# Reordering the prologue of a four-layer conditioned sequence kernel: which weights are loaded first, and what waits for them

## The reference

```python
# layer 0
x = x + a_alpha * attention(gamma * rmsnorm(x) + beta)          # 16 heads, softmax
x = x + f_alpha * (silu(h @ gate_w.T) * (h @ hidden_w.T) @ out_w.T + out_b)
# layer 1
u = (x * (scale * rsqrt(ms + EPS))) @ up_w.T; val, gate = split(u)
y = act_quant(val * gelu(gate)) @ weight_quant(down_w).T + x
#   weight_quant(w): s = 1/mean|w|; clip(round(w * s), -1, 1) / s
# layer 2
dWd = ((h_lang @ Wdd.T + bdd) * 0.1).reshape(B, 128, 256)       # per batch
dWu = ((h_lang @ Wdu.T + bdu) * 0.1).reshape(B, 256, 128)
x = x + relu(x @ (Wd + dWd).T + bd) @ (Wu + dWu).T + bu
# layer 3
out = (layernorm(x) * weight + bias + tanh(cond @ lin_w.T + lin_b)) * weight + bias
```

## Time and profile before

| | |
|---|---|
| median of 3 runs | 1004.62 us (1004.0 to 1006.42) |
| profiled execution | 1005.99 us |
| its span, first to last instruction | 1004.2 us |
| PE busy | 954.2 us, 95% of the span |
| VectorE, ScalarE, POOL busy | 745.1, 568.7, 230.8 us |
| mean granted TensorE clock | 0.98 |
| DMA | 89.43 MB, 89 GB/s over the span |

### The profile page before, as it was taken

One profiled execution on the slowest core, in us unless ns is written; L12 is line 12 of the kernel. 1 busy time (PEld: TensorE's weight loads), 2 busy tenths in 40 slices (PEclk: granted clock), 3 DMA queues, 4 the chain that ended last, 5 costly groups with the idle time before them and its releaser, 6 DMA issues.

```text
span 1004.2 us, 20848 instructions
## 1 busy us (share of the span) xinstructions
PE 954.2 (95%) x6574; PEld 782.9 (78%) x6574; DVE 745.1 (74%) x1728; ACT 568.7 (57%) x1167; POOL 230.8 (23%) x303
## 2 busy tenths in 40 slices
PE   6678799999999999999999999999999999998997
PEld 4346569788887979787888979787888979786776
DVE  3844368787878878787878878887878787885756
ACT  2365464756666564756665564746565564745542
POOL 1423502121121312221221312121212213111220
PEclk9789899999999999999999999999999999999999
DMA  8787742130404022130404021130404031120000
GB/s 276 247 284 288 264 166 62 44 106 3 148 1 137 11 85 62 43 105 1 147 1 139 9 95 52 48 100 1 147 1 142 6 104 44 54 84 2 22 16 17
DMA packets 76272, 89.43 MB, mean 89 GB/s; under 512 B 16512, under 2 KB 62864, under 8 KB 73616
## 3 DMA queue, kind: packets, MB, share of 16 engines
q1 hardware_dynamic: 70160, 63.07, 20.7%
q0 software_dynamic: 2304, 16.78, 4.6%
q10 hardware_dynamic: 3776, 9.18, 2.5%
HBM read 63.14 MB, written 25.31 MB: 88 GB/s over the span
## 4 chain that ended last, share of the span: by engine, by line
PE 83%; DVE 6%; DMA 4%; issue 3%; ACT 2%; POOL 0%; SPq 0%; ACTq 0%; DVEq 0%; POOLq 0%
PE bank L709 17%; PE bank L773 14%; PE bank L723 8%; PE bank L668 7%; PE bank L678 6%; PE bank L650 6%; PE bank L623 5%; PE bank L686 3%; PE bank L790 3%; PE bank L632 2%; DMA hyper<-w_hyper 2%; PE bank L602 2%; PE bank L810 1%; PE bank L783 1%; PE bank L695 1%
## 5 line engine op out<-in xcount | busy, mean ns | idle before, releaser
L529 POOL TENSOR_TENSOR act_lo<-act_f,act_hi 128x256 fp32r<-128x256 f32 x120 | 88.3, 736 | 363.6 <-ACT act_hi L1144 363.6
L1412 DVE TENSOR_REDUCE neg_max<-bank 128x2 f32<-128x512 f32 x256 | 162.2, 684 | 0.1
L1101 ACT ACTIVATE probs<-bank 128x512 f32<-128x512 f32 x256 | 134.9, 602 | 26.1 <-PE bank L668 13.6
L1180 ACT ACTIVATE gelu_g<-bank,r 128x256 f32<-128x256 f32 x128 | 60.9, 477 | 94.0 <-PE bank L773 91.4
L709 PE MATMUL bank<-h_hi,gh_hi 128*128 128x256 f32 x512 | 103.4, 283 | 2.8 <-DVE h_lo L1475 2.8
L1138 ACT ACTIVATE silu_g<-bank 128x256 f32<-128x256 f32 x128 | 49.4, 386 | 99.2 <-PE bank L709 98.5
L709 PE MATMUL bank<-h_lo,gh_hi 128*128 128x256 f32 x512 | 103.0, 283 | 0.0
L709 PE MATMUL bank<-h_hi,gh_lo 128*128 128x256 f32 x512 | 102.6, 282 | 0.0
L1481 DVE TENSOR_TENSOR act_f<-bank,silu_g 128x256 f32<-128x256 f32 x128 | 53.8, 421 | 63.8 <-ACT silu_g L1138 63.8
L1144 ACT ACTIVATE act_hi<-act_f 128x256 fp32r<-128x256 f32 x128 | 53.6, 419 | 75.6 <-DVE act_f L1481 73.4
L709 PEld LDWEIGHTS bank<-h_hi,gh_hi 128*128 128x128 f32 x512 | 82.6, 188 | 11.9 <-issue 7.0
(11 more groups left out here) (208 smaller groups left out, 2017.3 us busy)
## 6 DMA issues: line engine op xcount, KB each, us to landing
hyper<-w_hyper POOLq DMA_DIRECT2D x16, 1024.0 KB, 7.1
q_stack<-q_dram SPq DMA_DIRECT2D x96, 128.0 KB
k_stack<-k_dram SPq DMA_DIRECT2D x96, 128.0 KB
q_dram<-probs SPq DMA_DIRECT2D x16, 512.0 KB, 2.8
k_dram<-probs SPq DMA_DIRECT2D x16, 512.0 KB, 2.8
x_res<-xT SPq DMA_DIRECT2D x16, 256.0 KB, 2.8
delta_dram<-hyper_s ACTq DMA_DIRECT2D x15, 256.0 KB, 2.8
out<-xc SPq DMA_DIRECT2D x15, 256.0 KB, 2.5
```

Of the source, the lines that this page charges most:

```text
L529: pool.tensor_tensor(act_lo[:, c % 3, :], act_f[:, c % 2, :], act_hi[:, c % 3, :].bitcast(F32), ALU.subtract).then_inc(g_lo.sem, 1)
L1101: act.activation(probs[:, h % SLOTS], halves(SCORE_BANKS[h]), ACT.Exp, scale=float(H / D) ** 0.5).then_inc(s_exp.sem, 1)
L1180: act.activation(gelu_g[:, n % 2, :], halves(7 - n % 2)[:, 1, :], ACT.Gelu, scale=r3[:, t:t + 1])\
L1412: dve.tensor_reduce(neg_max[:, qt, :, pair:pair + 1].rearrange("p a o -> p (a o)"), halves(n % 3), AX_X, ALU.max, negate=True).then_inc(ma ...
```

## The change

The work itself stays the same. What changes is the order, the queue or the engine:

- **SP's prologue.** The conditioning table is loaded in two pieces, first the 128 KB for the attention's gamma and beta, later the rest. Batch 1's input is loaded into `x1`, which is free at that time, behind the qkv weights. The down weights follow at once. `write_qk` of batch 1 comes ahead of the table's store and no longer waits for it.
- **Key stack of batch 0 on POOL** (`stack_k`, semaphore `first_k_dma`), beside the query stack on SP.
- **Wide weights.** Pieces 0 and 1 are loaded behind both stacks of batch 0; pieces 2 to 5 behind the row of maxima; pieces 8 to 15 by SP instead of POOL, 8 to 11 ahead of the row of maxima of batch 1 and 12 to 15 behind it. Their products stand at other places, and pieces 2, 12 and 13 are evicted by VectorE.
- **Gate weights.** Both are loaded behind the stacks of batch 0 instead of at 10 us. The high part of the first is made in run 0 ahead of the exponentials, the high part of the second by VectorE. The last up weight is loaded in run 1.
- **Row of maxima.** SP issues it in run 0 ahead of the residual input `x_res` and ahead of the wait for the table.
- **Norms.** VectorE normalises batch 0 ahead of the first table steps, and batch 1 ahead of the rest of the table. The sum over the down weights moves ahead of batch 1's norm, its use (mean and reciprocals) behind the 16 maxima of batch 0, and PE's sum over the partitions goes to bank 3.
- **PE.** 6 and 8 products into bank 2 that nobody reads (`keep_busy`) stand ahead of the first norm and behind the first conditioning products. Batch 1's mean stands ahead of the remaining conditioning products.

```diff
@@ -186 @@ landed, by_dve, by_act
-def use(n):
-    return n // 4 if n < 6 else 2 + (n - 6) // 2
+def landed(n):
+    if n >= EARLY + 2:
+        return hyper_late[n % 2].sem, 16 * ((n - EARLY) // 2)
+    return hyper_in[slot(n)].sem, 16 * (n // 4 + 1 if n < EARLY else 3)
+def by_dve(n):
+    return HYPER_DVE.index(n) + 1
+def by_act(n):
+    return len([m for m in range(n + 1) if m not in HYPER_DVE])
@@ -260 @@ semaphores and places
-cond_in, vec_in, small_in, qkv_in, wo_in = sem("cond_in"), sem("vec_in"), sem("small_in"), sem("qkv_in"), sem("wo_in")
+cond_in, cond_late, vec_in, small_in, qkv_in, wo_in = sem("cond_in"), sem("cond_late"), sem("vec_in"), sem("small_in"), sem("qkv_in"), sem("wo_in")
 tanh_act, table, ternary, abs_mm = sem("tanh_act"), sem("table"), sem("ternary"), sem("abs_mm")
-w_hi, w_lo = sem("w_hi"), sem("w_lo")
+w_hi, w_hi_dve, w_lo = sem("w_hi"), sem("w_hi_dve"), sem("w_lo")
 hyper_in = [sem(f"hyper_in{i}") for i in range(4)]
+hyper_late = [sem(f"hyper_late{i}") for i in range(2)]
 EARLY = 6
-BESIDE = (0, 2, 3, 5, 6, 8, 9)
-HYPER_DVE = range(3, 4)
+HYPER_DVE = (2, 12, 13)
+BESIDE = (1, 2, 4, 5, 7, 8)
@@ -288 @@ hyper_load, stack_k
     return cond_dram[:, bass.ds(bat(b), 1), first * DC:(last + 1) * DC].rearrange("p o k -> p (o k)")
+def hyper_load(eng, n):
+    if n >= 4:
+        eng.wait_ge(hyper_mm.sem, n - 3 if n < EARLY else n - 1)
+    eng.dma_start(hyper[slot(n)][:], w_hyper[:, n * HYW:(n + 1) * HYW]).then_inc(landed(n)[0], 16)
         .then_inc(hyper_out[n % 4].sem, 16)
+def stack_k(eng, count):
+    for a in range(2):
+        even = slice(64 * a, 64 * a + 32, 2)
+        odd = slice(64 * a + 1, 64 * a + 32, 2)
+        third = slice(64 * a + 32, 64 * a + 64, 2)
+        for rows_at, part in ((even, 0), (odd, 0), (third, 1)):
+            src = k_dram[:, part].rearrange("(m a r) n -> a r m n", a=2, r=DH)[a]
+            to = k_stack[rows_at].rearrange("r (m a) n -> r a m n", a=2)[:, a]
+            eng.dma_start(to.bitcast(F32), src).then_inc(count.sem, 16)
@@ -374 @@ SP, run
     load_x(nxt)
-if a:
+if a and a.follows():
@@ -400 @@ SP, run, ahead of the row of maxima
         .then_inc(adapt_dma.sem, 16)
+if starts(f):
+    for n in range(8, 12):
+        hyper_load(sp, n)
@@ -408 @@ SP, run, behind the row of maxima
                      max_rows[NPAIR * par:NPAIR * (par + 1), :].bitcast(F32)).then_inc(max_dma.sem, 16)
+if starts(a):
+    sp.wait_ge(cond_out.sem, 16)
+    load_res(a)
+if starts(f):
+    hyper_load(sp, 12)
+    hyper_load(sp, 13)
+    hyper_load(sp, 14)
+    sp.wait_ge(hyper_ev_dve.sem, by_dve(12))
+    hyper_store(sp, 12)
+    hyper_load(sp, 15)
+    sp.wait_ge(hyper_ev_dve.sem, by_dve(13))
+    hyper_store(sp, 13)
 if starts(a):
-    for n in HYPER_DVE:
-        sp.wait_ge(hyper_ev_dve.sem, n - HYPER_DVE[0] + 1)
-        hyper_store(sp, n)
+    sp.wait_ge(hyper_ev_dve.sem, by_dve(2))
+    hyper_store(sp, 2)
@@ -452 @@ SP, prologue
 sp.dma_start(cond_t[C:P, NB:2 * NB], condT).then_inc(cond_in.sem, 16)
-sp.dma_start(cond_w, w_cond).then_inc(cond_in.sem, 16)
+sp.dma_start(cond_w[:, 0:2 * D], w_cond[:, 0:2 * D]).then_inc(cond_in.sem, 16)
 sp.dma_start(w_qkv[:], w_qkvT.rearrange("(c p) n -> p c n", p=P)).then_inc(qkv_in.sem, 16)
+for c in range(DC):
+    sp.dma_start(x1[:, c, :], rows(batch_of(xT, Batch(1)))[:, c, :]).then_inc(x_ahead.sem, 16)
+sp.dma_start(cond_w[:, 2 * D:], w_cond[:, 2 * D:]).then_inc(cond_late.sem, 16)
+sp.dma_start(w_down.rearrange("p (c n) -> p c n", n=D), w_downT.rearrange("(c p) n -> p c n", p=P))\
+    .then_inc(down_in.sem, 16)
@@ -461 @@ SP, prologue
                  one_row).then_inc(init_dma.sem, 16)
-sp.dma_start(w_down.rearrange("p (c n) -> p c n", n=D), w_downT.rearrange("(c p) n -> p c n", p=P))\
-    .then_inc(down_in.sem, 16)
 sp.dma_start(w_o[:], w_oT.rearrange("(c p) n -> p c n", p=P)).then_inc(wo_in.sem, 16)
-sp.wait_ge(n1_dve.sem, n1_dve.at(Batch(0)))
-for c in range(DC):
-    sp.dma_start(x_in[:, c, :], rows(batch_of(xT, Batch(1)))[:, c, :]).then_inc(x_in_dma.sem, 16)
 stack_qk(Batch(0))
+sp.wait_ge(stack_dma.sem, stack_dma.at(Batch(0), 16 * 8))
+sp.wait_ge(first_k_dma.sem, 16 * 6)
+write_qk(Batch(1))
              par_t[:].rearrange("p b k c -> p b (k c)")).then_inc(cond_out.sem, 16)
-sp.wait_ge(cond_out.sem, 16)
-write_qk(Batch(1))
@@ -530 @@ POOL, run
         sum_a(nxt)
-    if starts(f) and c in BESIDE:
-        hyper_load(8 + BESIDE.index(c))
 low_part(4)
-pool.wait_ge(max_dma.sem, max_dma.at(a))
-for n in range(13, NHY):
-    hyper_load(n)
@@ -568 @@ POOL, prologue
-def hyper_load(n):
-    if n >= 4:
-        pool.wait_ge(hyper_mm.sem, n - 3 if n < EARLY else n - 1)
-    pool.dma_start(hyper[slot(n)][:], w_hyper[:, n * HYW:(n + 1) * HYW]).then_inc(hyper_in[slot(n)].sem, 16)
 pool.memset(k_stack[:].bitcast(F32), 0.0).then_inc(init_pool.sem, 1)
-pool.wait_ge(stack_dma.sem, stack_dma.at(Batch(0)))
-for n in range(3):
-    hyper_load(n)
+pool.wait_ge(init_dma.sem, 32)
+pool.wait_ge(qk_dram_w.sem, qk_dram_w.at(Batch(0)))
+stack_k(pool, first_k_dma)
+pool.wait_ge(stack_dma.sem, stack_dma.at(Batch(0), 16 * 8))
+pool.wait_ge(first_k_dma.sem, 16 * 6)
+for n in range(2):
+    hyper_load(pool, n)
+pool.wait_ge(max_dma.sem, max_dma.at(Batch(0)))
+for n in range(2, EARLY):
+    hyper_load(pool, n)
 low_part(1)
-pool.wait_ge(max_dma.sem, max_dma.at(Batch(0)))
-for n in range(3, EARLY):
-    hyper_load(n)
 low_part(2)
-pool.wait_ge(stack_dma.sem, stack_dma.at(Batch(1)))
+pool.wait_ge(stack_dma.sem, stack_dma.at(Batch(1), 16 * 8))
 for n in range(EARLY, EARLY + 2):
-    hyper_load(n)
+    hyper_load(pool, n)
@@ -636 @@ PE, max_scores
 if n == 0:
-    pe.wait_ge(stack_dma.sem, stack_dma.at(b))
+    pe.wait_ge(stack_dma.sem, stack_dma.at(b, 16 * 8))
+    if starts(b):
+        pe.wait_ge(first_k_dma.sem, 16 * 6)
@@ -867 @@ PE, run, columns
     max_scores(a, 15)
-if starts(a) and c in (6, 8, 9):
-    hyper_product((6, 8, 9).index(c))
+if starts(a) and c >= FC:
+    hyper_product(c - FC)
@@ -886 @@ PE, run, parts t
         pe.wait_ge(x2_dve.sem, x2_dve.at(f))
+    if starts(a) and t == 2:
+        pe.wait_ge(ternary.sem, 2)
 if starts(a) and t >= 2:
-    hyper_product(1 + t)
-if starts(f) and t >= 2:
+    hyper_product(t)
+if starts(f) and t in (1, 2):
@@ -904 @@ PE, run
     ln_mean(g)
+if starts(f):
+    hyper_product(14)
     hyper_product(15)
+if starts(a):
+    hyper_product(4)
@@ -1020 @@ PE
+def keep_busy(n):
+    for _ in range(n):
+        pe.matmul(bank[2][:, 0:P], mean_w[:], mean_w[:], start=True, stop=True)
 pe.wait_ge(consts.sem, 4)
+keep_busy(6)
@@ -1033 @@ PE, prologue
 cond_products((0, 1), bank[3])
+keep_busy(8)
 project_v(Batch(0), 1)
+norm_a(Batch(1))
+pe.wait_ge(cond_late.sem, 16)
 cond_products(range(2, 8), bank[5])
-norm_a(Batch(1))
+pe.wait_ge(ternary.sem, 1)
+pe.matmul(bank[3][:, 511:512], ones[:], w_abs, start=True, stop=True).then_inc(abs_mm.sem, 1)
 project_qk(Batch(1), second=True)
-pe.wait_ge(table.sem, TABLE - 1)
-pe.wait_ge(ternary.sem, 1)
-pe.matmul(bank[5][:, 0:1], ones[:], w_abs, start=True, stop=True).then_inc(abs_mm.sem, 1)
@@ -1216 @@ ACT, run
 def run(a, f, g, nxt):
-    if starts(a):
-        hyper_out_piece(0)
@@ -1233 @@ ACT, run
         high_part(2 + c // 2)
-    if starts(f) and c in BESIDE and c < FC:
+    if starts(f) and c == 0:
+        raw_load(4)
+    if starts(f) and c in BESIDE[:5]:
     hyper_out_piece(11)
-    hyper_out_piece(12)
 if starts(a):
+    hyper_out_piece(0)
     hyper_out_piece(1)
-    hyper_out_piece(2)
+    high_part(0)
@@ -1252 @@ ACT, run
             exps(a, h)
-if starts(f):
-    hyper_out_piece(13)
     den_guess(a, 1)
-if starts(f):
-    hyper_out_piece(14)
 if starts(f):
+    hyper_out_piece(14)
 if starts(a):
+    hyper_out_piece(3)
@@ -1280 @@ ACT, run
 if starts(a):
-    act.wait_ge(stack_dma.sem, stack_dma.at(nxt))
+    act.wait_ge(stack_dma.sem, stack_dma.at(nxt, 16 * 8))
     raw_load(3)
-    raw_load(4)
@@ -1351 @@ ACT, prologue
-act.wait_ge(qkv_in.sem, 16)
-raw_load(0)
-raw_load(1)
 copy_v(Batch(0))
-square_a(Batch(1))
+square_a(Batch(1), x1)
+guess_a(Batch(1))
 act.preload_act_table_set("natural_log_exp_and_others")
-guess_a(Batch(1))
-high_part(0)
 split_qk(Batch(1), second=True)
-high_part(1)
+act.wait_ge(stack_dma.sem, stack_dma.at(Batch(0), 16 * 8))
+act.wait_ge(first_k_dma.sem, 16 * 6)
+raw_load(0)
+raw_load(1)
@@ -1601 @@ DVE
     dve.wait_ge(hyper_mm.sem, n + 1)
-    dve.wait_ge(hyper_out[n % 4].sem, 16 * (n // 4))
+    if n >= 4:
+        dve.wait_ge(hyper_out[n % 4].sem, 16 * (n // 4))
 def ternary_down():
+    dve.wait_ge(abs_mm.sem, 1)
+    dve.tensor_scalar(w_mean, bank[3][:, 511:512], 1.0 / (F * D), 1e-5, ALU.mult, ALU.max).then_inc(ternary.sem, 1)
+    dve.wait_ge(ternary.sem, 2)
+    dve.reciprocal(w_rec, w_mean).then_inc(ternary.sem, 1)
+    dve.wait_ge(ternary.sem, 3)
+    dve.reciprocal(down_scale[:], w_rec).then_inc(ternary.sem, 1)
@@ -1637 @@ DVE, run
 ternary_down()
+dve.wait_ge(raw_in[1].sem, 16)
```

(25 more changed lines are left out.)

50 lines of the change are left out of this document (25 added, 25 removed).

## The result

The changed kernel takes 999.99 us (996.25 to 1001.92, six executions) against 1005.52 us (1003.15 to 1009.05) for the kernel before: ratio 0.9938, 95% interval 0.9918 to 0.9958. It is faster, by 5.5 us, but 988.6 was forecast, and the result lies above the top of the range (999.0).

What follows compares the result with a forecast made beforehand. Late transfers were taken to bound the stages before the third run (155.79 us). Successive gains, some given back, moved it 16.0 us earlier to 139.8: 990.0 for the profiled execution, 988.6 for the median; range 983.5 to 999.

Steps and rivals of the forecast that it cites:

- First projection and POOL's issues: Batch 0's first projection starts at 10.7 and takes 3.7 us; POOL's key-stack issues cost 0.6 us each.
- The rival of a slow POOL: POOL issues the key stack's 1 KB-row transfers slowly; at 3.3 us an issue the 16.0 are used up; chance 0.03.
- Stacking: Batch 0's twelve key and query stack transfers take 8.2 us, landing at 28.1 against 35.89; gain 7.8.
- Batch 1's split: Other condition of the first maxima: batch 1's projection takes 3.7 us, split done at 27.4 to 28.4.
- Row and crowd: Run 0, first maxima (28.4) to first exponential (47.0): row lands 42.2 to 42.7, second wide weight 42.0; gain 7.2.
- Rest of run 0: First exponential to first gate keeps its lengths, gate at 74.5; out weights issued at 47 land by 57.
- Run 1: First gate to batch 1's scores takes 30.4 us against 38.33, without weight waits; gain 7.8 more, scores at 105.0.
- What is late next: Phrase from batch 1's split step: if the clock is low there, 1.7 us more.
- Residual behind the row: Residual load and table wait moved behind the row of maxima on SP: cost nothing if x_res lands before 65.
- Scores to projection: Batch 1's scores to its output projection take 18.1 us against 19.06; projection at 123.1, gain 16.0.
- The key stack behind 31 and the first exponential behind 50: Signs the forecast is wrong: key stack landing behind 31 us (forecast 28.1), or first exponential behind 50 (forecast 47).
- the loads still pace run 1: Rival: run 1's 6.4 us of weight waits and 3.4 of low clock stay; gain 6.2, time 998.4; chance 0.15.

Runs made afterwards that it cites:

- one_later: Changed kernel with par_f loaded earlier, plus second wide weight loaded behind the row of maxima and its product behind scores 12 to 15: 997.02 us, ratio 0.9899.
- prod_later: Changed kernel with the first two wide products behind scores 8 to 11, their evictions and first high part among the exponentials: 1000.15 us, ratio 0.9929.
- raw_early: Changed kernel with the first two gate weights (2 MB) issued at about 10 us again, instead of behind the stack: 1004.96 us, ratio 0.9991.

## Why the prediction was wrong

- **First projection and POOL's issues: right.** 10.43 and 3.69; 0.56 us an issue. The rival of a slow POOL is refuted. The keys were issued at 16.25, 17.18 and 16.78 (forecast 15.9), and the stack's first issue came 0.5 to 1.4 us late.
- **Stacking: a step that failed.** It scaled 211 GB/s at a busy share of 0.72 up to 293 GB/s at 1. The share is not a reserve: with 1.08 the rate is 196. The transfer took 10.4 to 10.9 us instead of 8.2, whoever issues it. By the Trainium skill (DMA: Bandwidth & Descriptors, Issuing engines are not separate DMA queues) a second issuer saves issue time alone; the prediction's estimate from that sentence was a stack at 26.5. The trace shows less still, 0 to 0.5 us of the 4.1 that the key issues take on SP. The stack came 2.7 to 4.0 us later than forecast.
- **Batch 1's split: the step that failed beside it.** The sum gave its projection 3.7 us, full clock, and kept 1.7 us for a low clock out of the sum. It took 6.71, 6.58 and 5.38 us at granted clocks of 0.54, 0.56 and 0.68, so the split was done at 31.3, 31.2 and 29.7 instead of 27.4 to 28.4. VectorE's reductions, which pace this stage, began at 31.2, 32.4 and 32.1, where the sum has them at 28.9 (0.5 us behind the first maximum, as before). Of these 2.3 to 3.5 us the stack alone is 0, 1.1 and 2.4; the rest the split would have cost with the stack in time.
- **Row and crowd: right but for 0.7 us.** 18.6 us were forecast from the first maxima to the first exponential and 19.3 to 19.4 measured. The row took 4.7 to 4.9 us to land, not 3.3, and the second wide weight came at 45.1 to 46.4. The mechanism was the one named: `one_later` takes the weight out, and the exponential comes at 46.8.
- **Rest of run 0: right in length, 27.1 to 28.0 against 27.5,** but it was covered less well than the prediction said. "The out weights, issued at 47, land by 57" was wrong by 8 to 12 us: they land 17 to 20 us behind the issue. In `one_later` and `prod_later` the exponentials came earlier and the first gate did not.
- **Run 1: the step that failed by the largest amount.** 30.4 was forecast; 32.6, 36.7 and 37.2 were measured (two of three over the 34 at which the prediction called itself wrong), and 30.0 to 31.6 in the three traces of kernels in which only the parameters (and the out weights) were moved. The sum left out one wait: the 3 KB of `par_f`, 0.6 us late before the change. It makes ScalarE wait 4.8 and 5.5 us and PE 4.0 and 4.1, and the granted clock is low behind that, which costs PE another 2.6 and 1.9 us. "What is late next" was asked of wide weights and ScalarE's instructions, not of the small loads behind them on SP. In the fastest execution the load landed after 8.9 us, in time, and its 2.2 us over the forecast come with the low clock at the start of the run. With the load moved the median is 996.4, inside the range.
- **Residual behind the row: priced at nothing, worth some 2 us** by one pair of kernels. The sum had this gain inside the row's 42.2 without saying so; the landing of the table, 14.4 us, was not looked at.
- **Scores to projection: 18.7 to 19.1 against 18.1. From there: right**, 16.6 to 16.7.

So of the 16 us, 6.0 were missing in the fastest execution and 11.1 to 11.5 in the other two. Of these, 6.0 to 6.6 are PE's wait for what the parameters held up and the slower work behind it. The key stack behind 31 and the first exponential behind 50, two more signs of being wrong that the prediction named, were met in the same two executions and missed narrowly in the fastest. The rival "the loads still pace run 1" had the nearest number (998.4) with another load as its cause: the wide weights made PE wait 1.1 us or less in run 1.

What stays open: why the same small load lands after 8.9 us in one execution and 12.6 in another, what sets the granted clock at the start of run 1 (0.61 in the fastest execution of the changed kernel, 1.00 in the other two), and what part of the first gate's spread (75.8 to 78.6) is the out weights.

## What to carry to other kernels

When a change takes a long wait away, list every load that lands in the same stretch and its distance to its reader, the small ones too: a 3 KB row issued behind megabytes lands with them (after 8.9 to 12.6 us here). Where two conditions release a step together, both need a bound in the sum: curing one shows the other. A DMA busy share below 1 with rows of 1 KB is not spare rate; test it by moving one stream to another queue. If the stages are all fed by transfers, an earlier start gains only as far as the next load is earlier too.

## What the hardware showed

- Twelve transfers of 1 KB rows: 188 GB/s at a DMA busy share of 0.69 from one queue, 196 to 221 at 1.05 to 1.10 from two.
- An issue can be held up: SP's issue of a small load took 3.54 us instead of 0.43 while 2 MB more were in flight (one trace, `raw_early`).
- A wait costs PE its clock as well: behind a wait of 4.0 us the granted clock was 0.54 for 6.4 us, and run 1 had 31.7 us of PE work instead of 29.1.
- VectorE's 512-column step from SBUF to bf16 took 5.59 instead of 0.43 us beside POOL's subtractions though it began 0.3 us ahead of them, and ended 0.3 us behind the last of the four. The Trainium skill (SBUF — State Buffer, Who interferes with whom) says that the port pair of the two is locked for a whole instruction and not shared; the row agrees that one of them stands, but here it stood through four POOL instructions (one trace, `one_later`).
